# Layer-0 attention of a two-layer graph kernel: scores once, with queries on partitions, instead of twice

## Chip, cores and metric

One core of a Trainium2 chip. The metric is the device time of one execution of the whole kernel, in microseconds (us); lower is better. Engines are named as in the profile: PE (TensorE matmuls; PEld its weight loads), DVE (VectorE), ACT (ScalarE), POOL (GpSimd), SP (the queue that issues the DMAs).

## The reference, cut to what matters

Sixteen samples of 512 nodes and 256 features go through two layers. Layer 0 is masked attention with 8 heads of 32, a residual and a layer norm; layer 1 is attention with one head whose logits are a sum of a query part and a key part.

```python
q, k, v = proj(Wq, bq), proj(Wk, bk), proj(Wv, bv)           # x @ W.T + b, 8 heads of 32
scores = einsum('bhqd,bhkd->bhqk', q, k) / sqrt(32)
scores = where(adj + eye > 0, scores, -inf)
out = einsum('bhqk,bhkd->bhqd', softmax(scores), v)          # -> (b, n, 256)
h = layernorm(x + out @ Wo.T + bo) * gamma + beta
f = h @ fc_w.T + fc_b                                        # layer 1
logits = (f @ q_w.T + q_b) + (f @ k_w.T + k_b).T
masked = logits + (1 - adj) * -1e9
masked = where(masked >= 0, masked, 0.01 * masked)
y = softmax(masked) @ f + h
```

## The kernel before, in words

Every matrix that must be exact to float32 is split in a high and a low part of type float32r; a product of two such is three matmuls (`three_terms`, L387). The 32 columns of a head's q and k are stacked three times on partitions by SBUF-to-SBUF DMAs (`stack`, L272, into `q_stack` and `k_stack`: high, low and high against high, high and low), so that one matmul of 96 rows gives the exact scores of a head.

Layer 0 computes the scores twice. A first pass (L534, `sm_bank`) has queries on partitions, in one float32r term, from a copy of q with the other heads' rows at zero (`q_pad`, filled by DMAs); DVE adds the mask and takes the maximum of each query's row (L928, one instruction and the read of its accumulator). The maxima are turned on PE (`turn_max`), negated and sent by DMA to a 97th row of `q_stack`. The second pass (L524 or L521, `st_bank`) has keys on partitions and the maximum already subtracted by that row; the mask is added by a bfloat16 matmul with a turned mask (L526) or, in 5 of 32 tiles, by DVE (L921); ACT takes the exponential (L708) into `e`, where it is already the moving operand for the product with v (`times_v`, L462, float32, four heads side by side, 32 columns of the array each). The sums of the exponentials run over partitions: POOL adds the four key tiles (`add_e`, L1009), PE multiplies the sum by ones (`total`, L472), DVE takes reciprocals of 128x512 (L856) and POOL multiplies the head outputs by them (L1014) and forms their low part (L1018).

Both passes have 32 tiles of 128x512 a sample (8 heads by 4 blocks of 128), two PSUM banks each; the product with v has one, and three banks are shared in turn by all else. The order of everything is written out by hand: each engine runs a loop over t (one step for each sample, with one step before and two after), in it a loop over 32 positions s. A position has one tile of either pass and the pieces placed there; a piece has an offset, as (15, "op0", -1) for the output projection of the sample before. The maxima of a sample run 21 tiles ahead of its exponentials (`LEAD`), the attention of layer 1 runs two samples behind. Engines take their instructions strictly in order and wait for each other by semaphores whose counts follow from these lists (`Signal`).

In one position PE runs:

```python
nc.tensor.matmul(bank, k_stack[g][:, i, kt*P:(kt+1)*P], q_stack[g][:, i, :], start=True, stop=False)  # L524
nc.tensor.matmul(bank, ident_b, mask_t[par][:, kt, :], start=False, stop=True)                         # L526
nc.tensor.matmul(sm_bank[s % 2], q_pad[j//GH][:, j%GH, qt*P:(qt+1)*P], kt_hi[j//GH], ...)              # L534
```

L526 and L534 are followed by the pieces of that position: transposes of x, of the normalised h and of layer 1's exponentials (L399, L481, L495), the projections q, k, v, op (output) and fc, the key logits kb (all L387), the product with v, the sums, the turned mask (L439) and layer 1's product (`attend`, L505). Other lines in the rows: ACT's copies out of PSUM (L651), its copies with a bias (L674), layer 1's exponential with the sum of its row (L646); POOL's layer-1 mask (L1047); DVE's small reciprocal (L941).

Of the kernel before, what the change touches and what calls it, by code (L numbers as in the profile page):

```python
# [29 lines left out]
P = 128  # L30
# [6 lines left out]
POS = NG * NT * GH  # L37
# [7 lines left out]
DVE_MASKED = (12, 14, 15, 26, 29)  # L45
LEAD = 21

FIRST, LAST = -1, NB + 1


def on(t, off):

    return 0 <= t + off < NB


class Signal:
# [9 lines left out]
    def after(self, step, t):  # L66
        last = self.place[step]
        return self.by * sum(min(max(t + off + (n <= last), 0), NB) for n, off in enumerate(self.offs))

PE_STEPS = [
# [6 lines left out]


OFF = {name: off for _, name, off in PE_STEPS}
FILLS = [name for _, name, _ in PE_STEPS if not name.startswith("pv")]
# [6 lines left out]
    "at1": ("dve", "fin1"), **{f"et{c}": ("act", f"et{c}") for c in range(NT)},  # L90
    **{f"m{j}": ("dve", f"m{j}") for j in range(NG)}}
ACT_STEPS = [
# [5 lines left out]
DVE_STEPS = [  # L98
# [5 lines left out]
POOL_STEPS = [  # L104
    ("sum1_3a", -1), ("sum1_3b", -1), ("x_bo", -1), ("o_norm0", -1), ("diag", 1), ("sum0_1a", 0), ("o_lo0", -1),
    ("sum0_1b", 0), ("sum0_2a", 0), ("sum0_2b", 0), ("o_norm1", -1), ("l_mask", -1), ("o_lo1", -1), ("sum0_3a", 0),
    ("sum0_3b", 0), ("neg_mean", -1), ("var_eps", -1), ("rstd", -1), ("shift", -1), ("sum1_1a", 0), ("sum1_1b", 0),
    ("h_gamma", -1), ("h_rest", -1), ("sum1_2a", 0), ("sum1_2b", 0)]


def maxima_tile(s):

    n = s - (POS - LEAD) if s >= POS - LEAD else s + LEAD
    return (1 if s >= POS - LEAD else 0), n // NT, n % NT


def build(nc, x, adj, wq, bq, wk, bk, wv, bv, wo, bo, gamma, beta, fc_w, fc_b, q_w, q_b, k_w, k_b, out):
    with ExitStack() as ctx:  # L118
# [24 lines left out]
        ident_b = sb("ident_b", [P, P], BF16)  # L143
        ones = sb("ones", [P, DH])
# [9 lines left out]
        mask_t = [sb(f"mask_t{i}", [P, NT, N], BF16) for i in range(2)]  # L154
# [7 lines left out]
        q_stack = [sb(f"q_stack{g}", [STACK + 1, GH, N], F32R) for g in range(NG)]  # L162
        k_stack = [sb(f"k_stack{g}", [STACK + 1, GH, N], F32R) for g in range(NG)]
        v = sb("v", [P, NT, D])
        row_max = sb("row_max", [P, NH, NT])
        neg_max = sb("neg_max", [GH * NT, NG, P], F32R)
        e = sb("e", [P, NT, GH, N])
        e_sum = sb("e_sum", [P, GH, N])
        q_pad = [sb(f"q_pad{g}", [P, GH, N], F32R) for g in range(NG)]
# [3 lines left out]


        o_raw = [sb("o_raw0", [P, N]), x_in[:, 2:4, :].rearrange("p c d -> p (c d)")]
        recip = [sb("recip0", [P, N]), x_in[:, 0:2, :].rearrange("p c d -> p (c d)")]
# [7 lines left out]
        rstd = sb("rstd", [P, NT])  # L184
        feat = sb("feat", [P, NT, D])
        z = sb("z", [P, NT, N + 2])
        scratch = e[:, :, :, :].rearrange("p c g n -> p (c g) n")
# [52 lines left out]
        def program(iteration):  # L240

            for t in range(FIRST, LAST + 1):
                iteration(t, t % 2)
# [855 lines left out]
```

## Time and profile before

| | |
|---|---|
| median of 3 runs (lowest, highest) | 1097.93 us (1094.98, 1108.29) |
| the profiled execution, its own time | 1106.9 us |
| its span, first to last instruction | 1104.8 us |
| mean granted TensorE clock | 0.971 of 2.4 GHz |
| instructions | 16668 |
| DMA, mean of the 16 engines | 109 GB/s |

The busy time of PE is a union of modelled durations: a matmul's duration has its way through the array in it, and the next one starts before it ends. What a stretch of matmuls costs is therefore read as the difference of two start times. The same holds in part for ACT and DVE, where an instruction starts some 0.1 us before the one ahead of it has ended.

### The profile page before, as it was taken

To read this page: it belongs to the slowest core of one execution; us is meant where nothing else is said; L and a number is where in the kernel's file an instruction comes from. 1 tells how busy PE (TensorE), PEld (TensorE's weight loads), DVE (VectorE), ACT (ScalarE), POOL (GpSimd) and SP (SyncE) were. 2 spreads that over 40 slices of the span, in tenths; PEclk is the share of its full clock that TensorE was granted. 3 is DMA by queue.
4 is the path that set the end of the run, shared out by engine and by line. 5 is a ranking of instruction groups with operands and counts; after the bars stand their busy time and mean duration, and the time that the engine had idled before them with its cause. 6 is when DMAs were issued, how large, how long until landed. Compare 5 with 4: busy or idle time off the path is not lost. (4 is left out here: it accounts for less than half of the span.)

```text
span 1104.8 us, 16668 instructions
## 1 busy us (share of the span) xinstructions
PE 1021.8 (92%) x5720; PEld 649.2 (59%) x5720; DVE 782.6 (71%) x1945; ACT 622.8 (56%) x1180; POOL 722.8 (65%) x415
## 2 busy tenths in 40 slices
PE   5789899999999999999999998999999999999866
PEld 4445565656656565665666564666656566665454
DVE  4667777877767787777778777777767767775432
ACT  2145466565646557575655657564555746566633
POOL 3056787675667667666777766576766657778740
PEclk9899999999999999999999999999989999999978
DMA  5677827576564667667374767646366663745010
GB/s 133 106 123 145 133 73 143 102 144 96 113 116 89 135 113 144 96 121 127 102 134 83 153 115 137 103 103 119 79 141 105 136 108 99 135 76 90 29 48 28
DMA packets 81571, 120.89 MB, mean 109 GB/s; under 512 B 9296, under 2 KB 36432, under 8 KB 81488
## 3 DMA queue, kind: packets, MB, share of 16 engines
q1 hardware_dynamic: 81488, 119.84, 56.8%
q8 instruction: 46, 0.75, 0.3%
q14 instruction: 37, 0.30, 0.1%
HBM read 52.44 MB, written 8.39 MB: 55 GB/s over the span
## 5 line engine op out<-in xcount | busy, mean ns | idle before, releaser
L708 ACT ACTIVATE e<-st_bank 128x512 f32<-128x512 f32 x512 | 307.4, 602 | 404.1 <-PE st_bank L526 223.5
L928 DVE CUSTOM_DVE_ANT_0 sm_bank<-sm_bank,masks 128x512 f32<-128x512 f32 x512 | 354.1, 693 | 155.3 <-PE sm_bank L534 152.2
L1009 POOL TENSOR_TENSOR e_sum<-e_sum,e 128x1024 f32<-128x1024 f32 x128 | 303.7, 2385 | 49.8 <-ACT e L708 49.8
L534 PE MATMUL sm_bank<-kt_hi,q_pad 128*128 128x512 f32 x512 | 281.9, 552 | 32.9 <-issue 28.0
L524 PE MATMUL st_bank<-q_stack,k_stack 97*128 97x512 f32 x432 | 197.7, 458 | 3.8 <-ACT e L708 3.0
L1009 POOL TENSOR_TENSOR e_sum<-e 128x1024 f32<-128x1024 f32 x64 | 152.2, 2378 | 67.9 <-ACT e L708 61.1
L526 PE MATMUL st_bank<-mask_t,ident_b 128*128 128x512 bf16 x432 | 169.2, 392 | 0.0
L524 PEld LDWEIGHTS st_bank<-q_stack,k_stack 97*128 97x128 f32 x432 | 81.5, 189 | 111.5 <-ACT e L708 103.3
L462 PE MATMUL o_bank<-e,v 128*32 128x512 f32 x1024 | 136.4, 605 | 0.7 <-ACT e L708 0.7
L505 PE MATMUL shared<-feat,z 128*128 128x256 f32 x512 | 134.5, 412 | 1.4 <-ACT z L651 1.4
L534 PEld LDWEIGHTS sm_bank<-kt_hi,q_pad 128*128 128x128 f32 x512 | 103.2, 202 | 44.5 <-issue 31.8
L505 PEld LDWEIGHTS shared<-feat,z 128*128 128x128 f32 x512 | 105.7, 209 | 18.7 <-ACT z L651 2.2
L526 PEld LDWEIGHTS st_bank<-mask_t,ident_b 128*128 128x128 bf16 x432 | 42.0, 97 | 81.7 <-issue 73.4
L1034 POOL TENSOR_SCALAR_AFFINE_SELECT masks<-masks 128x512 bf16<-128x512 bf16 x16 | 10.2, 639 | 119.8 <-DVE masks L911 119.8
L921 DVE TENSOR_TENSOR st_bank<-st_bank,mask_t 128x512 f32<-128x512 f32 x80 | 56.0, 701 | 34.8 <-PE st_bank L521 33.7
L387 PE MATMUL shared<-weight_hi,split_hi 128*128 128x256 f32 x256 | 73.7, 288 | 6.0 <-POOL split_lo L1018 6.0
L387 PE MATMUL shared<-weight_hi,split_lo 128*128 128x256 f32 x256 | 72.7, 284 | 0.0
L928 DVE DVE_READ_ACCUMULATOR2_ANT row_max<- 128x1 f32 x512 | 72.6, 142 | 0.0
L387 PE MATMUL shared<-weight_lo,split_hi 128*128 128x256 f32 x256 | 72.6, 283 | 0.0
L856 DVE RECIPROCAL recip<-recip 128x128 f32<-128x128 f32 x64 | 60.5, 946 | 12.8 <-ACT recip L651 12.7
L856 DVE RECIPROCAL x_in<-x_in 128x128 f32<-128x128 f32 x64 | 60.2, 945 | 4.5 <-ACT x_in L651 4.5
L387 PE MATMUL shared<-xt_hi,weight_hi 128*128 128x512 f32 x128 | 53.2, 416 | 2.5 <-DVE xt_lo L838 1.8
(131 smaller groups left out, 1836.7 us busy)
## 6 DMA issues: line engine op xcount, KB each, us to landing
adj_in<-in_adj SPq DMA_DIRECT2D x32, 1024.0 KB, 7.8
q_stack<-qt_hi SPq DMA_DIRECT2D x64, 256.0 KB, 9.7
k_stack<-kt_hi SPq DMA_DIRECT2D x64, 256.0 KB, 8.8
x_in<-in_x SPq DMA_DIRECT2D x16, 512.0 KB, 10.4
q_pad<-qt_hi SPq DMA_DIRECT2D x128, 64.0 KB, 7.7
q_stack<-qt_lo SPq DMA_DIRECT2D x32, 256.0 KB, 8.6
k_stack<-kt_lo SPq DMA_DIRECT2D x32, 256.0 KB, 11.9
h<-in_x SPq DMA_DIRECT2D x16, 512.0 KB, 3.8
```

The lines of the kernel that those rows point to most:

```text
L387: last = nc.tensor.matmul(bank, a, b, start=(kt == 0 and n == 0), stop=(kt == kts - 1 and n == 2))
L462: last = nc.tensor.matmul(o_bank[i * DH:(i + 1) * DH, :], v[:, kt, o:o + DH], e[:, kt, i, :], start=(kt == 0), stop=(kt == NT - 1))
L505: last = nc.tensor.matmul(bank[:, k * D:(k + 1) * D], z[:, c, kt * P:(kt + 1) * P], feat[:, kt, :], start=(kt == 0), stop=(kt == NT - 1))
L524: nc.tensor.matmul(bank[:, :], k_stack[g][:, i, kt * P:(kt + 1) * P], q_stack[g][:, i, :], start=True, stop=False)
L526: nc.tensor.matmul(bank[:, :], ident_b[:, :], mask_t[par][:, kt, :], start=False, stop=True).then_inc(st_done.sem, 1)
L534: nc.tensor.matmul(sm_bank[s % 2][:, :], q_pad[j // GH][:, j % GH, qt * P:(qt + 1) * P], kt_hi[j // GH][:, :], start=True, stop=True).then ...
L708: nc.scalar.activation(e[:, kt, i, :], st_bank[s % 2][:, :], ACT.Exp, scale=SCALE)\
L856: last = nc.vector.reciprocal(recip[g][:, n], recip[g][:, n])
L921: nc.vector.tensor_tensor(st_bank[s % 2][:, :], st_bank[s % 2][:, :], mask_t[par][:, kt, :], ALU.add)\
L928: nc.vector.tensor_tensor_reduce(sm_bank[s % 2][:, :], sm_bank[s % 2][:, :], mask[nxt if off else par][:, qt * N:(qt + 1) * N], 1.0, LOWES ...
L1009: nc.gpsimd.tensor_tensor(e_sum[:, pair, :], a, b, ALU.add).then_inc(pool_done.sem, 1)
L1034: nc.gpsimd.affine_select(out=mask_diag[nxt], in_=mask_diag[nxt], compare_op=ALU.not_equal, fill=0.0, base=0, pattern=[[0, NT], [-1, P]], ...
```

## The change

- The scores are computed once, as tiles of 128 queries by 512 keys, exact, from the stacks of 96 rows (the 97th row, `q_pad`, the first pass, the mask matmul, the turned mask and the turned maxima go). The weights and the bias of q carry -1/sqrt(32), so the masked minimum is taken.
- DVE adds the mask and takes the minimum of each row in place; ACT computes exp(min - x) with a bias from a column and sums each row as it goes (`accum_out`); DVE takes the reciprocal of 128 sums; POOL multiplies the tile by them; PE turns the tile, four float32 transposes of 128x128; ACT (22 of 32) or DVE (10 of 32) copies it to `e_t`. The distances: reciprocal one position behind, transposes and copy three behind; `e` holds four tiles, the scores have two banks, the turned tiles two, the shared ones stay three.
- The product with v runs four times a sample, each over 4 key tiles and 4 heads with 256 queries, where it ran eight times over 4 heads with 512. Its result is already normalised: ACT makes the high part from its bank, DVE the low part. `add_e`, `total`, the 128x512 reciprocals and POOL's two steps go.
- Steps of POOL on h (residual bias, gamma, rest) and its layer-1 mask are cut in four.
- All pieces are placed anew, by position and offset in one number (position = number mod 32, samples behind = number div 32).

```diff
+TURN = 3
+ROOM = 4
+RECIP = 1
+SCORED = 2
+TURNED = 2
+SHARED = 3
+DVE_COPIED = (0, 1, 2, 4, 12, 13, 22, 25, 29, 31)
+PE_AT = {
+    "v1": 0, "v0": 2, "et0": 67, "pv3": 37, "et3": 71, "xt0": -25, "at2": 71, "at3": 73, "xt1": -23, "op0": 42,
+    "op1": 43, "et1": 76, "q0": -20, "at0": 77, "at1": 79, "k0": -16, "ht1": 50, "ht0": 50, "pv0": 18, "fc0": 51,
+    "fc1": 53, "kb": 54, "pv1": 23, "k1": -7, "q1": -3, "pv2": 30, "et2": 63}
+SP_AT = {
+    "x": -32, "stack1": 1, "store1": 66, "store0": 73, "x_again": 15, "stack0": -13, "adj": -12, "adj_again": 24}
...
+            def scores(s, b):
+                g, i, qt = tile(s)
+                if s % (TILES // NG) == 0:
+                    pe.wait_ge(stacked[g].sem, stacked[g].of(f"stack{g}", b))
+                u, earlier = ago(s, SCORED)
+                pe.wait_ge(exp_done.sem, exp_done.of(u, b + earlier))
+                nc.tensor.matmul(sm_bank[(TILES * b + s) % SCORED][:, :], q_stack[g][:, i, qt * P:(qt + 1) * P], k_stack[g][:, i, :],
+                                 start=True, stop=True).then_inc(sm_done.sem, 1)
+            def turn(u, b):
+                pe.wait_ge(scaled.sem, scaled.of(u, b))
+                w, earlier = ago(u, TURNED)
+                copied = dve_copied if w in DVE_COPIED else act_copied
+                pe.wait_ge(copied.sem, copied.of(w, b + earlier))
+                n = TILES * b + u
+                for c in range(NT):
+                    last = nc.tensor.transpose(et_bank[n % TURNED][:, c * P:(c + 1) * P], e[:, n % ROOM, c * P:(c + 1) * P], ident[:, :])
+                last.then_inc(turned.sem, 1)
...
+            def exponential(s, b):
+                u, earlier = ago(s, ROOM)
+                act.wait_ge(min_done.sem, min_done.of(s, b))
+                act.wait_ge(turned.sem, turned.of(u, b + earlier))
+                n = TILES * b + s
+                k = n % ROOM
+                nc.scalar.activation(e[:, k, :], sm_bank[n % SCORED][:, :], ACT.Exp, scale=-1.0, bias=row_min[:, k:k + 1],
+                                     accum_out=row_sum[:, k:k + 1]).then_inc(exp_done.sem, 1)
...
+            def masked_minima(s, b):
+                qt = tile(s)[2]
+                if s == 0:
+                    dve.wait_ge(pool_done.sem, pool_done.of("diag", b))
+                dve.wait_ge(sm_done.sem, sm_done.of(s, b))
+                n = TILES * b + s
+                bank, k = sm_bank[n % SCORED], n % ROOM
+                nc.vector.tensor_tensor_reduce(bank[:, :], bank[:, :], mask[b % 2][:, qt * N:(qt + 1) * N], 1.0, -LOWEST,
+                                               ALU.add, ALU.min, row_min[:, k:k + 1])\
+                    .then_inc(min_done.sem, 1)
+            def reciprocal(u, b):
+                dve.wait_ge(exp_done.sem, exp_done.of(u, b))
+                k = (TILES * b + u) % ROOM
+                nc.vector.reciprocal(row_recip[:, k:k + 1], row_sum[:, k:k + 1]).then_inc(recip_done.sem, 1)
...
+            def normalise(s, b):
+                pool.wait_ge(recip_done.sem, recip_done.of(s, b))
+                k = (TILES * b + s) % ROOM
+                nc.gpsimd.tensor_scalar(e[:, k, :], e[:, k, :], row_recip[:, k:k + 1], None, ALU.mult).then_inc(scaled.sem, 1)
```

In a position PE runs the scores, then the transposes of three tiles before, ACT the copy of three before, then the exponential, DVE the minimum, then the reciprocal of one before and the copy of three before, with the pieces of the position between or after them.

## Rows read from the trace of the kernel before

**Rows 1.** The page, part 1: busy us and share of each engine.

```profile
PE 1021.8 (92%) x5720; PEld 649.2 (59%) x5720; DVE 782.6 (71%) x1945; ACT 622.8 (56%) x1180; POOL 722.8 (65%) x415
```

**Rows 2.** Windows: busy us of each engine, granted clock, DMA share, GB/s.

```profile
182.00:243.00 61.00, 59.79 (x350) 37.55 (x348) 47.63 (x119) 38.44 (x73) 42.70 (x25) 1.00 0.61 110
...
792.00:853.00 61.00, 58.17 (x313) 35.51 (x312) 43.82 (x109) 35.68 (x68) 38.74 (x23) 0.94 0.62 116
...
1036.00:1105.00 69.00, 43.45 (x218) 33.24 (x216) 21.51 (x60) 26.62 (x54) 26.30 (x17) 0.85 0.13 42
```

**Rows 3.** Timeline of PE, one tile: start us, duration us, instruction.

```profile
511.71 0.39 PE L524 MATMUL st_bank<-q_stack,k_stack 97*128 97x512 f32 x1
511.94 0.39 PE L526 MATMUL st_bank<-mask_t,ident_b 128*128 128x512 bf16 x1
511.98 0.59 PE L534 MATMUL sm_bank<-kt_hi,q_pad 128*128 128x512 f32 x1
512.41 0.28 PE L387 MATMUL shared<-weight_hi,split_hi 128*128 128x256 f32 x1
```

**Rows 4.** Timeline of PE, four float32 transposes and a layer-1 product.

```profile
525.38 0.60 PE L481 MATMUL shared<-ident,h 128*128 128x128 f32 x4
525.82 1.89 PE L505 MATMUL shared<-feat,z 128*128 128x256 f32 x8
527.36 0.59 PE L524 MATMUL st_bank<-q_stack,k_stack 97*128 97x512 f32 x1
```

**Rows 5.** Timeline of PE, the product of four heads with v.

```profile
516.71 1.07 PE L462 MATMUL o_bank<-e,v 128*32 128x512 f32 x8
517.71 0.50 PE L524 MATMUL st_bank<-q_stack,k_stack 97*128 97x512 f32 x1
```

**Rows 6.** Lines by form: busy us, mean ns of one, idle us.

```profile
L472 PE MATMUL shared<-e_sum,ones 128*32 128x512 f32 x256 | 34.1, 605 | 1.4 <-POOL e_sum L1009 1.4
L1047 POOL TENSOR_SCALAR adj_in<-adj_in 128x2048 f32<-128x2048 f32 x16 | 30.4, 1900 | 3.2 <-DMA adj_in<-in_adj 1.9
L1014 POOL TENSOR_TENSOR x_in<-x_in 128x512 f32<-128x512 f32 x16 | 20.4, 1272 | 5.2 <-DVE x_in L856 5.2
```

**Rows 7.** Timeline of ACT: copy, copy with bias, exponential with a sum.

```profile
511.57 0.58 ACT L651 COPY z<-shared 128x512 f32<-128x512 f32 x1
512.04 0.71 ACT L674 ACTIVATE qt_hi<-shared,bias_col 128x512 fp32r<-128x512 f32 x1
512.62 0.61 ACT L708 ACTIVATE e<-st_bank 128x512 f32<-128x512 f32 x1
...
551.33 0.76 ACT L646 ACTIVATE z<-z,l_negmax 128x512 f32<-128x512 f32 x1
...
552.04 0.64 ACT L708 ACTIVATE e<-st_bank 128x512 f32<-128x512 f32 x1
```

**Rows 8.** Timeline of DVE: masked maximum and a small reciprocal.

```profile
503.80 0.69 DVE L928 CUSTOM_DVE_ANT_0 sm_bank<-sm_bank,masks 128x512 f32<-128x512 f32 x1
...
504.41 0.17 DVE L941 RECIPROCAL l_recip<-l_sum 128x4 f32<-128x4 f32 x1
```

**Rows 9.** Timeline: first, third, sixteenth sample, last tile, last output projection.

```profile
53.52 0.47 PE L524 MATMUL st_bank<-q_stack,k_stack 97*128 97x512 f32 x1 [0.16 <-issue]
...
161.73 0.60 ACT L708 ACTIVATE e<-st_bank 128x512 f32<-128x512 f32 x1 [0.29 <-PE st_bank L526]
...
992.72 0.60 ACT L708 ACTIVATE e<-st_bank 128x512 f32<-128x512 f32 x1 [0.29 <-PE st_bank L526]
...
1044.51 0.50 PE L524 MATMUL st_bank<-q_stack,k_stack 97*128 97x512 f32 x1
...
1062.02 0.39 PE L387 MATMUL shared<-weight_hi,split_hi 128*128 128x256 f32 x1 [1.23 <-POOL split_lo L1018]
```

**Rows 10.** Timeline of SP, then its DMA to landing, first 60 us.

```profile
32.60 0.60 SPq L278 DMA_DIRECT2D k_stack<-kt_lo  x1
...
k_stack<-kt_lo SPq DMA_DIRECT2D x2, 256.0 KB, 12.8
```

More of the change, by code:

```diff
@@ L64, in __init__, with of, all @@
         assert len(self.place) == len(steps)
-    def after(self, step, t):
+    def of(self, step, b):
         last = self.place[step]
+        t = b - self.offs[last]
         return self.by * sum(min(max(t + off + (n <= last), 0), NB) for n, off in enumerate(self.offs))
-PE_STEPS = [
[6 rows of a table removed]
-OFF = {name: off for _, name, off in PE_STEPS}
-FILLS = [name for _, name, _ in PE_STEPS if not name.startswith("pv")]
+    def all(self, name, b):
+        return max(self.of(step, b) for step in self.place if step[:-1] == name and step[-1].isdigit())
+FILLS = [name for name, _ in steps(PE_AT) if not name.startswith("pv") and name not in ("at1", "at3")]
+BANK = {name: n % SHARED for n, name in enumerate(FILLS)}
+BANK["at1"], BANK["at3"] = BANK["at0"], BANK["at2"]
 READ_BY = {
@@ L223, in build @@
[L223 to L224 removed]
+        shared = [pb(f"shared{i}") for i in range(SHARED)]
+        bank_of = {name: shared[n] for name, n in BANK.items()}
+        tiles = [(s, 0) for s in range(TILES)]
+        sm_done = Signal(sem("sm_done"), tiles)
+        min_done = Signal(sem("min_done"), tiles)
+        exp_done = Signal(sem("exp_done"), tiles)
@@ new lines, in build @@
+        recip_done = Signal(sem("recip_done"), [ago(s, RECIP) for s in range(TILES)])
+        scaled = Signal(sem("scaled"), tiles)
+        turned_tiles = [ago(s, TURN) for s in range(TILES)]
+        turned = Signal(sem("turned"), turned_tiles)
+        act_copied = Signal(sem("act_copied"), [u for u in turned_tiles if u[0] not in DVE_COPIED])
+        dve_copied = Signal(sem("dve_copied"), [u for u in turned_tiles if u[0] in DVE_COPIED])
+        pe_done = Signal(sem("pe_done"), steps(PE_AT))
@@ new lines, in times_v, with turn_h @@
+                        last = nc.tensor.matmul(o_bank[i * DH:(i + 1) * DH, 2 * half * P:2 * (half + 1) * P], v[:, kt, o:o + DH],
+                                                e_t[:, k % 2, kt, i, :], start=(kt == 0), stop=(kt == NT - 1))
+                last.then_inc(pe_done.sem, 1)
+            def turn_h(kt, b):
+                pe.wait_ge(act_done.sem, act_done.all("hn", b))
+                pe.wait_ge(*bank_read(f"ht{kt}", b))
+                bank = bank_of[f"ht{kt}"]
+                for c in range(NT):
+                    last = nc.tensor.transpose(bank[:, c * P:(c + 1) * P], h[b % 2][:, c, kt * P:(kt + 1) * P], ident[:, :])
+                last.then_inc(pe_done.sem, 1)
@@ new lines, in attend @@
+            def attend(c, b):
+                k = c % 2
+                pe.wait_ge(act_done.sem, max(act_done.of(f"et{c}", b), act_done.all("feat", b)))
+                if k == 0:
+                    pe.wait_ge(*bank_read(f"at{c}", b))
+                bank = bank_of[f"at{c}"]
+                for kt in range(NT):
+                    last = nc.tensor.matmul(bank[:, k * D:(k + 1) * D], z[:, c, kt * P:(kt + 1) * P], feat[:, kt, :],
+                                            start=(kt == 0), stop=(kt == NT - 1))
+                last.then_inc(pe_done.sem, 1)
@@ new lines, in o_high, with normal_rows @@
+            def o_high(g, b):
+                act.wait_ge(pe_done.sem, max(pe_done.of("kb", b - 1), pe_done.all("fc", b - 1)))
+                copy(o_hi[:, g, :], f"pv{2 * g + 1}", o_bank[:, :], b)
+            def normal_rows(half, b):
+                act.wait_ge(pool_done.sem, pool_done.of("shift", b))
+                for c in range(2 * half, 2 * half + 2):
+                    last = nc.scalar.activation(h[b % 2][:, c, :], h[b % 2][:, c, :], ACT.Identity, bias=shift[:, c:c + 1],
+                                                scale=rstd[:, c:c + 1])
+                last.then_inc(act_done.sem, 1)
@@ new lines, in query_logits @@
+            def query_logits(half, b):
+                dve.wait_ge(act_done.sem, act_done.of(f"feat{half}", b))
+                dve.wait_ge(pe_done.sem, pe_done.all("at", b - 1))
+                for k in range(2):
+                    c = 2 * half + k
+                    last = nc.vector.tensor_tensor_reduce(z[:, c, 0:D], bank_of[f"fc{half}"][:, k * D:(k + 1) * D], qw_row[:, :],
+                                                          1.0, logit_bias[:, 3:4], ALU.mult, ALU.add, q_dot[:, c:c + 1])
+                last.then_inc(done, 1)
```

1162 lines of the change are left out of this document (516 added, 646 removed), and 29 rows, old and new, of tables (ACT_AT, ACT_STEPS, DVE_AT, DVE_STEPS).

## Prediction

> **What bounds the kernel now.** I read the page first: PE is busy 1021.8 of 1104.8 us, 92%, DVE 71%, POOL 65%, ACT 56% [rows 1]. Then the windows: in a full stretch of 61 us at clock 1.00 PE is busy 59.8, DVE 47.6, POOL 42.7, ACT 38.4 [rows 2]. PE sets the pace. Its durations overlap, so I worked from start times. Tile starts: L524 at 511.71, the piece behind its three matmuls at 512.41, so a tile with the mask matmul costs 0.70 us back to back, about 0.235 a matmul of 512 columns [rows 3]. A layer-1 product of eight instructions costs 1.54, four transposes 0.44 [rows 4], four heads' product with v 1.00 [rows 5], and the sums over partitions are of the same form (605 ns, 8 instructions) [rows 6]. For a sample: 27 tiles at 0.75 (0.70, and some have an entry from a float32 group) and 5 at 0.50 make 22.8; q and k 24 matmuls at 0.235, 5.6; v, op and fc 72 half-width ones at 0.118, 8.5; kb 6 at 0.235, 1.4; layer 1's product 4 x 1.54, 6.2; its, x's and h's 32 transposes at 0.11, 3.5; v-product 8 x 1.05 with its entries, 8.4; sums 2.1; turned mask and maxima about 1.1. Together 59.6. The samples are 63.9 us apart: the third sample's first exponential is at 161.73, the sixteenth's at 992.72, 830.99/13 [rows 9]. So 4.3 us a sample are waits and lower clock. The rest of the span: the first tile starts at 53.52, from the last tile (1044.51) to the end it is 60.3 us [rows 9].
>
> **The change on PE, where it counts.** Per sample it removes 32 score matmuls at 0.235 (7.5), 27 mask matmuls (6.3), the sums (2.1), the turned mask and maxima (1.1). It adds 128 float32 transposes. Four of them cost 0.44 from start to start [rows 4], so 32 x 0.44 = 14.1. The new position is then 0.235 + 0.44 = 0.68, 21.6 a sample against 22.8 for the old tiles. A switch from float32r scores to float32 transposes may cost more: at worst a score matmul has left the array before the next group starts, 0.39 instead of 0.235 [rows 3], which is 0.16 x 32 = 5.0 more. At best nothing. I take nothing, because groups of float32 and float32r follow each other in rows 4 with no such gap, and keep 5.0 for the range. The v-product has the same columns in 64 half-width steps: 4 heads, 512 columns, cost 1.00, so 256 cost 0.50 at least, 16 x 0.50 = 8.0 less shared entries, against 8.4; if weight loads of 32 columns don't hide under half the columns, each step costs up to 0.65, 2.4 more, the other end. I take 7.6. New sum: 21.6 + 5.6 + 8.5 + 1.4 + 6.2 + 3.5 + 7.6 = 54.4, 5.2 under the old.
>
> **ACT.** Removed: the copies of the sums, of the turned mask and of the head output. Added: the exponential gets a bias column and a sum. A plain copy holds ACT 0.47, one with a bias column 0.58, an exponential with bias and sum 0.71 (551.33 to 552.04, read from SBUF) [rows 7]; the plain exponential is of the first kind. So 0.60 to 0.71, I take 0.68: 32 x 0.68 = 21.8. 22 copies at 0.47, 10.3. The rest of its pieces (4 logits 2.6, 4 exponentials 2.8, 4 turned tiles 1.9, norm 2.0, ten copies 4.8, q and k 2.3) 16.4. Sum 48.5, from 36 to 38 of busy time before [rows 2].
>
> **DVE.** Minimum 0.61 from start to next start, its accumulator read beside it [rows 8]: 19.5. Ten copies at 0.61, 6.1; 32 reciprocals of one column, up to 0.17 each [rows 8], 4.5. Its other pieces add to 17: 47, as before (the large reciprocals and masked tiles go).
>
> **POOL.** 32 multiplications of 128x512 by a column. A tensor_scalar of four times the width takes 1.90, a tensor_tensor of this width 1.27 [rows 6], so 0.48 to 1.27; I take 0.6, the nearer kind, with a start cost. 19.2, with 13.5 for h, the mask and the norm 33, in place of 42. At 1.27 it would be 54, and nearly the bound.
>
> **What now waits.** The two score banks are the loop: scores(s) waits for exp(s-2). A round is matmul 0.5, minimum 0.61 + 0.14, exponential about 0.9 with its sum, four hand-overs at about 0.1: 2.5 to 2.6 us for two tiles. Behind that wait on PE stand the transposes and all pieces of the position. Where both positions are full PE needs 2.8 or more for two and the wait is over before; where neighbours are empty it needs 1.36. By the placement positions 26 to 28 are empty on PE and 3 and 4 nearly so: there PE waits about 1.3 and 1.0 us a sample. Single empty ones leave 0.2 to 0.3 for what ACT has ahead of the exponential (a copy, 0.47), another 1.2. Transposes come three positions behind (5.6 us), the chain to them takes about 4, so no wait as long as POOL takes 0.6. The clock and small waits I leave at 2. So 54.4 + 1.3 + 1.0 + 1.2 + 2 = 59.9, 60 us a sample.
>
> **SP.** Every DMA of `q_pad` (8 a sample) and of the maxima goes; the stacks, x, adj and stores stay. stack0 is issued at position 19 for the next sample, 13 positions or 24 us ahead; its six DMAs take 3.9 us to issue and up to 12.8 to land [rows 10]. stack1 has 15 positions. adj_again stands in SP from position 24 until the next masks are made at 31; behind it are only x and stack1 of the next turn. I cost this at nothing; if that cover went, the first scores of a head group would be late by what is missing of 17 us.
>
> **Ends.** The first tile no longer waits for maxima. It waits for stack0, whose last DMA is issued at 32.60 and lands in 12.8, at 45 [rows 10], against 53.52. The first two samples took 108.2 to 161.73 [rows 9]; without layer 1's and then the output's pieces the new loop gives 43 and 51, 94. The last sample, with nothing to prepare, 53 (before 51.8). The end: before, the last output projection starts at 1062.02 [rows 9], 17.5 after the last tile, with sum, reciprocals and POOL's two steps in it; now about 9.5 (transpose, copy, product, two halves). The 42.8 behind it stay. 52.3.
>
> Sum: 45 + 94 + 13 x 60 + 53 + 52 = 1024 against 1104.8; with the 2.1 us around the span 1026 against 1106.9. That execution lies 0.8% above the median, so for a median 1026 x 1097.9/1106.9 = 1018 us, 7.3% faster.
>
> **Rivals.** Time = (244 + 13 P + 2) x 0.992 with P the us between samples.
> (1) PE closes up: few waits, P = 57: 979 to 980 less 4 for lighter ends, about 975. For it: the other engines need under 49. Against: two banks and strict order.
> (2) The gain goes into the switch between scores and transposes: 5.0 a sample on PE, P = 65: 1082. For it: no row shows float32r scores straight before transposes of data that had long been there.
> (3) Slower, by the score loop: the exponential stands on ACT behind all that is placed there. The bare loop is 16 x 2.6 = 42 a sample; if ACT's 16.4 of pieces and half of DVE's 17 and half the ACT copies lie in it and not beside it, P = 42 + 16 + 8.5 + 5 = 71.5, 1166. It decides from a round of 3.75 us (2 x 60/32); equal to the kernel before at 4.0. Against: heavy PE positions give the others time.
> (4) Slower, by the clock. Transposes take 17.6 of 60 us, so the other matmuls only 37 to 38, 62%; in the window from 1036, where PE was busy 63% of the time, the clock was 0.85 [rows 2]. There 30% of the time is at 1.2 GHz, where half-width matmuls start 0.21 apart instead of 0.118. P = 54.4/(1 - 0.3 x 0.45) + 5 = 68: 1121. Against: the transposes here keep PE busy in time, and in rows 4 they run at full speed in their places. The Trainium skill ("TensorE: Matmul & The Clock Gate", Part 4: PE-mode transpose) says that transposes don't count as PE-busy in the way that brings the full clock, which is this rival; the trace has too few transposes to bear it out.
> (5) POOL's multiplication costs 1.27: P about 63: 1057.
> (6) The change doesn't do what it says, that is, the deleted matmuls weren't on the path. Rows 1 speak against it.
>
> **Chances.** Forecast (P 58.5 to 63, with rival 5 in it) 0.54; (1) 0.18; (2) 0.10; (3) 0.10; (4) 0.06; (6) 0.02. Likeliest 1018. The range from 965 (rival 1 with P = 56) to 1085 (rival 2) leaves (3) and (4) out, 0.16. This kernel can be told from no change at about 2%, 1076 us. Faster: 0.54 + 0.18 and part of (2) and (3), 0.77; same 0.11; slower 0.12.
>
> **What would show it.** Right: L534's successor and one matmul a tile on PE, starts of scores and transposes 0.68 apart when nothing waits; four transposes 0.44; exponentials 0.68 apart back to back; POOL at 0.6; first tile near 45; 60 between samples; PE busy near 90%, and its waits for exponentials at positions 26 to 28 and 4. Wrong: a clock under 0.95; transposes at 0.6 or more for four; PE waiting for exponentials at most positions; POOL above 1.0 and PE waiting for it; waits of PE for the stacks at positions 0 or 16.

## The result, and the profile after

The changed kernel takes 1145.7 us (four runs, 1144.6 to 1147.6), 1.040 times the time before, 95% interval 1.035 to 1.046: slower, where 1018 us was forecast in a range of 965 to 1085. The page of after, parts 1 and 4 (busy us and share of each engine; the chain of work that ended last, by engine), beside [rows 1]:

```profile
PE 979.0 (86%) x7304; PEld 770.4 (67%) x7304; DVE 763.9 (67%) x2412; ACT 824.6 (72%) x1948; POOL 1013.0 (88%) x856
...
POOL 61%; PE 24%; DVE 6%; issue 3%; ACT 2%; DMA 1%; SPq 1%; DVEq 0%; ACTq 0%
```

PE did get its work cut. But POOL, at 65% before, is now the busiest engine, and the last chain runs through it. The windows of after (columns as in [rows 2]):

```profile
182.00:243.00 61.00, 54.51 (x435) 43.07 (x434) 43.82 (x140) 47.69 (x115) 58.27 (x51) 1.00 0.54 110
...
792.00:853.00 61.00, 53.85 (x422) 42.53 (x420) 43.32 (x136) 46.69 (x112) 58.29 (x50) 0.97 0.55 113
```

In the first of these windows PE is busy 54.5 of 61 us, where it had 59.8, and POOL 58.3, where it had 42.7. What POOL does, in the lines by form of after:

```profile
L1013 POOL TENSOR_SCALAR e<-e,row_recip 128x512 f32<-128x512 f32 x512 | 805.0, 1581 | 52.7 <-DVE row_recip L888 45.9
L998 POOL TENSOR_TENSOR h<-h,gamma_row 128x256 f32<-128x256 f32 x64 | 46.7, 730 | 5.9 <-PE shared L449 4.1
...
L993 POOL TENSOR_SCALAR adj_in<-adj_in 128x512 f32<-128x512 f32 x64 | 39.6, 619 | 5.3
```

The multiplication of one tile takes 1581 ns; the layer-1 mask, also a tensor_scalar and of the same shape, takes 619. The waits (engine, line, releaser: us in total, times, longest) show who waits behind it:

```profile
DVE sm_bank L881 <- PE sm_bank L483: 204.3, 179, 11.0
PEld et_bank L493 <- POOL e L1013: 191.6, 218, 1.8
ACT e_t L652 <- PE et_bank L493: 123.6, 159, 3.7
PE et_bank L493 <- POOL e L1013: 120.8, 172, 1.6
```

PE's transposes wait for POOL, ACT's copies for PE, DVE's minima for the scores that stand behind those transposes on PE: one releaser, passed on. The timeline at the points of [rows 9]: the first sample's first scores, first exponential of the third and of the sixteenth sample, last scores, and last output projection:

```profile
44.58 0.79 PE L483 MATMUL sm_bank<-k_stack,q_stack 96*128 96x512 f32 x1 [11.34 <-DMA k_stack<-kt_lo]
...
165.65 0.69 ACT L660 ACTIVATE e<-sm_bank,row_min 128x512 f32<-128x512 f32 x1 [1.91 <-DVE row_min L881]
...
1029.20 0.69 ACT L660 ACTIVATE e<-sm_bank,row_min 128x512 f32<-128x512 f32 x1 [1.65 <-DVE row_min L881]
...
1091.44 0.50 PE L483 MATMUL sm_bank<-k_stack,q_stack 96*128 96x512 f32 x1
...
1106.48 0.47 PE L385 MATMUL shared<-weight_hi,split_hi 128*128 128x256 f32 x1
```

The samples are (1029.20 - 165.65)/13 = 66.4 us apart, where 60 was forecast and 63.9 measured before. Put together by the forecast's own terms: start 44.6, first two samples 121.1, thirteen at 66.4, last 62.2, end 53.3, together the span of 1144.7.

### The profile page after: what moved, and what is told of

Read it like the earlier page. It is cut to its first block, busy times and chain, and to the rows that moved or that the text cites. A ratio compares the mean times of both kernels' runs of the same rounds, so it can differ in the third digit from the quotient of the medians.

```text
span 1144.7 us, 22568 instructions
## 1 busy us (share of the span) xinstructions
PE 979.0 (86%) x7304; PEld 770.4 (67%) x7304; DVE 763.9 (67%) x2412; ACT 824.6 (72%) x1948; POOL 1013.0 (88%) x856
## 4 chain that ended last, share of the span: by engine, by line
POOL 61%; PE 24%; DVE 6%; issue 3%; ACT 2%; DMA 1%; SPq 1%; DVEq 0%; ACTq 0%
POOL e L1013 48%; PE shared L385 10%; PE et_bank L493 6%; POOL h L998 3%; PE shared L473 3%; POOL h L1003 3%; POOL adj_in L993 2%; DVE sm_bank L881 2%; POOL h L973 2%; PE sm_bank L483 2%; DVE z L864 2%; POOL rstd L985 1%; PE shared L449 1%; DMA k_stack<-kt_lo 1%; PE shared L463 1%
## 5 line engine op out<-in xcount | busy, mean ns | idle before, releaser
L1013 POOL TENSOR_SCALAR e<-e,row_recip 128x512 f32<-128x512 f32 x512 | 805.0, 1581 | 52.7 <-DVE row_recip L888 45.9
L493 PE MATMUL et_bank<-ident,e 128*128 128x128 f32 x2048 | 326.1, 282 | 123.2 <-POOL e L1013 120.8
L660 ACT ACTIVATE e<-sm_bank,row_min 128x512 f32<-128x512 f32 x512 | 357.8, 702 | 64.4 <-DVE row_min L881 61.5
L493 PEld LDWEIGHTS et_bank<-ident,e 128*128 128x128 f32 x2048 | 239.5, 143 | 214.8 <-POOL e L1013 191.6
L652 ACT COPY e_t<-et_bank 128x512 f32<-128x512 f32 x352 | 208.3, 592 | 123.7 <-PE et_bank L493 123.6
L483 PE MATMUL sm_bank<-k_stack,q_stack 96*128 96x512 f32 x512 | 249.7, 488 | 13.8 <-DMA k_stack<-kt_lo 11.3
L483 PEld LDWEIGHTS sm_bank<-k_stack,q_stack 96*128 96x128 f32 x512 | 98.8, 193 | 48.9 <-issue 25.1
L894 DVE COPY e_t<-et_bank 128x512 f32<-128x512 f32 x160 | 109.4, 684 | 26.4 <-PE et_bank L493 24.2
L440 PE MATMUL o_bank<-e_t,v 128*32 128x256 f32 x2048 | 125.5, 386 | 0.0
L660 ACT ACTIVATION_READ_ACCUMULATOR e<-sm_bank,row_min 128x1 f32 x512 | 108.2, 211 | 0.0
```

The costliest lines, as they stand in the source:

```text
L440: last = nc.tensor.matmul(o_bank[i * DH:(i + 1) * DH, 2 * half * P:2 * (half + 1) * P], v[:, kt, o:o + DH], e_t[:, k % 2, kt, i, :], start ...
L483: nc.tensor.matmul(sm_bank[(TILES * b + s) % SCORED][:, :], q_stack[g][:, i, qt * P:(qt + 1) * P], k_stack[g][:, i, :], start=True, stop=T ...
L493: last = nc.tensor.transpose(et_bank[n % TURNED][:, c * P:(c + 1) * P], e[:, n % ROOM, c * P:(c + 1) * P], ident[:, :])
L652: nc.scalar.copy(turned_to(u), et_bank[(TILES * b + u) % TURNED][:, :].rearrange("p (c n) -> p c n", c=NT)).then_inc(act_copied.sem, 1)
L660: nc.scalar.activation(e[:, k, :], sm_bank[n % SCORED][:, :], ACT.Exp, scale=-1.0, bias=row_min[:, k:k + 1], accum_out=row_sum[:, k:k + 1] ...
L894: nc.vector.tensor_copy(turned_to(u), et_bank[(TILES * b + u) % TURNED][:, :].rearrange("p (c n) -> p c n", c=NT))\
```

## Experiments

Each is an edit of the changed kernel, or of one that is named. "Period" is the time from one sample to the next in the profiled run, from the third sample's first exponential to the sixteenth's, divided by 13; the changed kernel has 66.4 us. "Idle time" is POOL's, in gaps over 0.1 us, for each sample. Times are medians, of four runs in most cases, of ten in e12 and e16 and of one in e5; the kernel before, measured anew beside them, took 1093 to 1101 us.

### What one multiplication costs, and what it decides

**e1: a constant in place of the column.**

```diff
-nc.gpsimd.tensor_scalar(e[:, k, :], e[:, k, :], row_recip[:, k:k + 1], None, ALU.mult)
+nc.gpsimd.tensor_scalar(e[:, k, :], e[:, k, :], 0.03125, None, ALU.mult)
```

> The changed kernel with GpSimd's multiplication of each tile of exponentials by a constant in the place of the column of reciprocals; it leaves out the softmax's division, and keeps every wait, transfer and place. Theory (GpSimd bounds the changed kernel, through 32 multiplications a sample of 1.58 us where the prediction had 0.6): one multiplication falls to about 0.62 us, GpSimd to some 35 us a sample, and the sample from 66.4 us to 57 to 60 us, what TensorE's own 54.4 us and its waits make; the whole execution to 1013 to 1055 us (14 periods shorter than 1144.7). Rival (the score loop over two banks and the new places of the pieces bound it, GpSimd's busy time is only a wait passed on): at most 1.5 us a sample less, 1125 us or more. Rival (GpSimd's column operand is not what is dear, any multiplication of this shape in place is): still 1.58 us each and 1145 us.

1159.0 us, 1.058 times before: that the column is what is dear is refuted, and the last rival holds (any multiplication of this shape in place is dear). The line of the multiplication in e1:

```profile
L1013 POOL TENSOR_SCALAR e<-e 128x512 f32<-128x512 f32 x512 | 769.9, 1504 | 81.7 <-DVE row_recip L888 44.6
```

Its recorded duration is a little shorter, but two in a row start 1.567 us apart (median), against 1.541 with the column. 32 x 0.026 = 0.8 us a sample more; the period went from 66.4 to 67.1. This is a first sign that the period follows POOL.

**e2: a product with the repeated column.**

```diff
+nc.gpsimd.tensor_tensor(e[:, k, :], e[:, k, :], row_recip[:, k:k + 1].to_broadcast([P, N]), ALU.mult)
```

> The changed kernel with the same multiplication written as a product of two tensors, the second one the reciprocal's column repeated along the row; computes the reference. Theory (a scalar operand read from a column is what is dear on GpSimd): the product takes about 1.27 us as GpSimd's other product of this shape did in the kernel before, so GpSimd has 32 x 1.3 + 15 = 57 us a sample, and the sample is 59 to 62 us, 1040 to 1085 us in all. Rival (any operation of GpSimd with a second operand is at the same pace here): 1.5 to 1.6 us each and 1135 to 1150 us. Rival (the bound is the score loop): 1125 us or more whatever it costs.

1007.1 us, 0.920 times before (0.912 to 0.928), below the range expected. It computes the same and takes 12% less than the changed kernel, by one instruction's form. Its line and a window:

```profile
L1013 POOL TENSOR_TENSOR e<-e,row_recip 128x512 f32<-128x512 f32 x512 | 537.1, 1053 | 175.4 <-DVE row_recip L888 170.1
```

```profile
182.00:243.00 61.00, 60.15 (x484) 49.28 (x477) 48.77 (x154) 53.01 (x128) 48.98 (x56) 1.00 0.61 124
```

POOL has fallen to 49.0 of 61 us and PE stands at 60.2: the bound is back at PE, the period is 58.0 us.

**e5: a price list.** Tile s of a sample is multiplied, added to or copied in form s mod 8, each on its own line.

```diff
+if s % 8 == 0:   last = nc.gpsimd.tensor_scalar(ek, ek, col, None, ALU.mult)                 # L1015
+elif s % 8 == 1: last = nc.gpsimd.tensor_scalar(ek, ek, col, 1.0, ALU.mult, ALU.mult)        # L1017
+elif s % 8 == 2: last = nc.gpsimd.tensor_scalar(ek, ek, 0.0, col, ALU.add, ALU.mult)         # L1019
+elif s % 8 == 3: last = nc.gpsimd.tensor_scalar(ek, ek, 0.0, 0.03125, ALU.add, ALU.mult)     # L1021
+elif s % 8 == 4: last = nc.gpsimd.tensor_scalar(ek, ek, 0.0, None, ALU.add)                  # L1023
+elif s % 8 == 5: last = nc.gpsimd.tensor_tensor(ek, ek, ek, ALU.mult)                        # L1025
+elif s % 8 == 6: last = nc.gpsimd.tensor_scalar(ek, ek, 0.5, 0.0625, ALU.mult, ALU.mult)     # L1027
+elif s % 8 == 7: last = nc.gpsimd.tensor_copy(ek, ek)                                        # L1029
```

> A price list: the changed kernel in which GpSimd treats its tiles in eight forms by turns, each on a line of its own, 64 of each: (0) times a column, one operation; (1) times a column, times 1.0; (2) plus 0.0, times a column; (3) plus 0.0, times a constant, the form of the layer-1 mask; (4) plus 0.0 alone; (5) the product of the tile with itself as two tensors; (6) times a constant, times a constant; (7) a copy. Forms 3 to 7 leave out the softmax's division. Known so far for 128x512: form 0 1.58 us, times a constant alone 1.50, tensor product with a repeated column 1.05, plus then times constants (on the adjacency) 0.62. Theory A (an instruction with one operation is slow, with two fast): forms 1, 2, 3, 6 near 0.62, form 4 at 1.5. Theory B (the first operation decides, a multiplication is slow): forms 0, 1, 6 at 1.5, forms 2, 3, 4 near 0.62. Theory C (this tile is slow, by what else reads and writes it, and the mask's tile is not): all forms at 1.0 to 1.6, form 3 too.

The lines by form of e5:

```profile
L1015 POOL TENSOR_SCALAR e<-e,row_recip 128x512 f32<-128x512 f32 x64 | 100.6, 1572 | 43.5 <-DVE row_recip L888 43.5
L1023 POOL TENSOR_SCALAR e<-e 128x512 f32<-128x512 f32 x64 | 98.2, 1534 | 40.1 <-DVE row_recip L888 40.1
L1025 POOL TENSOR_TENSOR e<-e 128x512 f32<-128x512 f32 x64 | 73.0, 1141 | 7.6 <-DVE row_recip L888 7.6
L1017 POOL TENSOR_SCALAR e<-e,row_recip 128x512 f32<-128x512 f32 x64 | 44.5, 695 | 1.9 <-DVE row_recip L888 0.3
L1019 POOL TENSOR_SCALAR e<-e,row_recip 128x512 f32<-128x512 f32 x64 | 44.5, 695 | 12.5 <-DVE row_recip L888 10.8
L1027 POOL TENSOR_SCALAR e<-e 128x512 f32<-128x512 f32 x64 | 39.8, 622 | 10.1 <-DVE row_recip L888 7.3
L1021 POOL TENSOR_SCALAR e<-e 128x512 f32<-128x512 f32 x64 | 39.8, 621 | 62.4 <-DVE row_recip L888 62.4
L1029 POOL COPY e<-e 128x512 f32<-128x512 f32 x64 | 39.2, 612 | 57.2 <-DVE row_recip L888 57.1
```

Theory A (the number of operations decides) holds alone. Both tensor_scalar lines with one operation take over 1.5 us, addition and multiplication alike; all four with two take 0.62 to 0.70. By recorded durations a column in place of a constant costs 0.04 to 0.07 more; with one operation the distance of starts (e1) doesn't bear that out. It is not the tile, since the same tiles are quick in other forms, and not the kind of operation. Why one operation is the slow form no run here shows.

**e7: the same multiplication in two operations.**

```diff
-nc.gpsimd.tensor_scalar(e[:, k, :], e[:, k, :], row_recip[:, k:k + 1], None, ALU.mult)
+nc.gpsimd.tensor_scalar(e[:, k, :], e[:, k, :], row_recip[:, k:k + 1], 1.0, ALU.mult, ALU.mult)
```

> The changed kernel with each multiplication as one instruction of two operations, times the column, times 1.0; computes the reference. Theory A (one operation slow, two fast): about 0.7 us each, GpSimd 37 us a sample; TensorE's 54.4 us and its waits on the scores and on ACT stay, and the period is 56.5 to 58 us, 985 to 1007 us in all. Theory B or C (the operation or the tile decides): 1.5 to 1.6 us each, 1140 to 1160 us.

990.6 us, 0.905 times before (0.899 to 0.910), 13.5% less than the changed kernel: the best of all. Its line, and its window in which PE is busy 60.45 of 61 us:

```profile
L1013 POOL TENSOR_SCALAR e<-e,row_recip 128x512 f32<-128x512 f32 x512 | 370.3, 724 | 323.6 <-DVE row_recip L888 319.4
```

```profile
182.00:243.00 61.00, 60.45 (x482) 50.35 (x482) 49.91 (x165) 53.91 (x129) 38.23 (x56) 1.00 0.63 122
```

The period is 57.0 us. POOL has 38.2 of 61 us and waits for the reciprocals; ACT, the next busiest after PE, has 53.9.

### Does POOL's time count one for one?

**e6: the cheaper form of e2 in 8 of 32 tiles** (`if s % 4 == 1`).

> The changed kernel with 8 of a sample's 32 multiplications (every fourth tile, from tile 1) as a product with the repeated column, the other 24 as they were; computes the reference. The two forms start the next instruction 1.541 and 0.996 us later, so GpSimd has 8 x 0.545 = 4.4 us a sample less. Theory (GpSimd's own time sets the sample's period one for one, until TensorE takes over at 58.0 us): 66.4 - 4.4 = 62.0 us a sample, 1145 - 14 x 4.4 = 1083 us, 1075 to 1092. Rival (as three tiles taken off GpSimd gave a third of their time only, the period follows at a third): 64.9 us, 1124 us.

1083.3 us, period 62.4: 4.0 of 4.4 us counted, as the theory had it.

**e3: three multiplications (tiles 5, 15, 26) on VectorE**, behind the reciprocal; PE's transposes wait for the engine that did the tile.

```diff
+DVE_SCALED = (5, 15, 26)
...
+nc.vector.tensor_scalar(e[:, k, :], e[:, k, :], row_recip[:, k:k + 1], None, ALU.mult).then_inc(dve_scaled.sem, 1)
```

> The changed kernel with 3 of a sample's 32 multiplications (tiles 5, 15 and 26) on VectorE, right behind the reciprocal, and the other 29 on GpSimd as they were; computes the reference. Theory (GpSimd is the bound, so its time comes off one for one): the sample gets 3 x 1.55 = 4.7 us shorter, 61.8 us, and the whole 1075 to 1090 us. Rival (the score loop): less than 1.5 us a sample, 1125 us or more; were VectorE's or ACT's chain the bound, the three operations added to VectorE would make it longer, 1145 us or more.

1125.6 us, period 64.9: 1.5 of 4.7 us. The theory missed; the result lies at the very edge of the rival (1125 or more), though POOL, not the score loop, is what PE still waits for. **e4: the sixteen odd tiles there.**

> The changed kernel with every second multiplication (the odd tiles) on VectorE, right behind the reciprocal; computes the reference. Theory: GpSimd falls to 16 x 1.55 + 15 = 40 us a sample and bounds nothing; VectorE has 43.1 us and 16 operations of 0.3 to 0.6 us more, 48 to 53 us, under TensorE's 54.4 us, so the sample is 57 to 60 us and the whole 1013 to 1055 us. Rival (score loop): 1125 us or more. Rival (VectorE pays as much for a column operand as GpSimd): VectorE has 68 us and the kernel takes 1165 us or more.

1049.6 us, 0.959 times before, in the expected range; the period of 60.5 lies a little above the 57 to 60 expected. VectorE is busy 87% of the span and takes 658 ns for a multiplication, where 300 to 600 was assumed.

**e8: e3 with tiles 6, 18 and 30.** They were chosen by POOL's idle time behind each tile, over eight samples (2.1 us a sample in the changed kernel, 5.1 in e3).

> As the run with three one-operation multiplications on VectorE, but of tiles 6, 18 and 30 in place of 5, 15 and 26; computes the reference. There the trace had GpSimd idle 5.2 us a sample against 2.3 before, 1.7 of it ahead of the product with gamma that stands behind tile 15 and waits for TensorE, 0.9 behind tile 4. Theory (GpSimd's time counts one for one where it has a backlog, and is lost where its next piece waits for another engine): the idle time stays near 2.3 us, the sample gets 4 to 4.6 us shorter, 62 us, and the whole 1080 to 1092 us. Rival (VectorE's added work is what ate two thirds of the gain, wherever the tiles are): 64.9 us and 1125 us again.

1134.5 us, period 65.7: theory and rival both missed, the choice was worse, and the idle time 5.9 us. **e14: the same three multiplied by no engine.**

> The changed kernel in which tiles 6, 18 and 30 are not multiplied by any engine (their softmax's division is left out); the other 29 are multiplied on GpSimd in one operation as before. GpSimd has 4.6 us a sample less, as when VectorE did these three (65.6 us a sample, 1134 us). Theory (the ring over three tiles keeps GpSimd from running ahead, whoever does the three): little better than 1134 us, 1115 to 1135. Rival (VectorE's three operations of 0.66 us, each ahead of a minimum, gave the gain back): 61.8 to 62.5 us a sample, 1080 to 1092 us.

1131.7 us, period 65.6, the same as e8's: VectorE's added work isn't what ate the gain. **e15: the same three on POOL, in two operations.**

> The changed kernel with tiles 6, 18 and 30 multiplied on GpSimd as all others, but in the form of two operations; computes the reference. GpSimd has only 3 x (1.54 - 0.70) = 2.5 us a sample less, not 4.6 as when VectorE did them. Theory (time taken off GpSimd counts one for one while it stays within what the ring lets it run ahead): 63.9 us a sample, 1110 us, 1100 to 1118, better than with the same three on VectorE (1134). Rival (these three places are no good for a gain, or each gain counts at a third): 65.6 us, 1130 us or more.

1133.7 us, period 65.8: only 0.6 of 2.5 us; the theory missed, its rival on the places holds. **e16: e15 with tiles 1, 13 and 25.**

> The changed kernel with the two-operation form in tiles 1, 13 and 25, in place of tiles 6, 18 and 30 (1134 us, 65.7 us a sample, GpSimd's idle time up from 2.3 to 3.9 us); computes the reference. In the run with the cheaper form in every fourth tile from tile 1, GpSimd's idle time did not grow behind tiles 1, 13 and 25. Theory (a cut counts in full at tiles behind which the next reciprocals are long made, and is lost where the ring is tight already): idle time near 2.3 us, 66.4 - 2.5 = 63.9 us a sample, 1105 to 1116 us. Rival (three single cuts are lost in any place, a cut counts only when spread evenly): 65.5 us and 1130 us or more.

1097.7 us, period 63.45: 3.0 us for a cut of 2.5, idle time 1.7. The same cut, in other places, takes four times as much off the whole (48 us against 12). The timeline of e15 at tile 18 shows how a cut is lost (L1014 is the two-operation form):

```profile
596.97 0.28 PE L385 MATMUL shared<-weight_hi,split_lo 128*128 128x256 f32 x1
...
597.80 0.40 PE L483 MATMUL sm_bank<-k_stack,q_stack 96*128 96x512 f32 x1
597.83 0.70 POOL L1014 TENSOR_SCALAR e<-e,row_recip 128x512 f32<-128x512 f32 x1
...
598.23 0.70 DVE L881 CUSTOM_DVE_ANT_0 sm_bank<-sm_bank,masks 128x512 f32<-128x512 f32 x1 [1.31 <-PE sm_bank L483]
...
598.85 0.16 DVE L888 RECIPROCAL row_recip<-row_sum 128x1 f32<-128x1 f32 x1
...
599.11 1.57 POOL L1016 TENSOR_SCALAR e<-e,row_recip 128x512 f32<-128x512 f32 x1 [0.57 <-DVE row_recip L888]
```

POOL is done with tile 18 at 598.5, but the reciprocal of tile 19 is only started at 598.85: on VectorE it stands behind the minimum of tile 20, which waited 1.31 us for scores that stood on PE behind a projection. It is a ring: multiplication of a tile, its transposes, the scores four tiles on, their minimum, the reciprocal of the tile before them, and that tile's multiplication, three tiles after the first. Where PE has a long piece in it, one turn is longer than POOL's own work: here from tile 16 (started at 593.92) to tile 19 it took 5.2 us, of which POOL was busy 4.4. The trace of the changed kernel tells the good places beforehand: there the reciprocal of the tile behind each cut of e16 (tiles 2, 14 and 26) had been ready for 1.75, 2.39 and 1.52 us when POOL came to it, of the tile behind each cut of e15 (7, 19 and 31) for 1.00, 0.39 and 0.09, and of tile 8 for 0.28 (means of eight samples). One cut is 0.84 us. Two sets of three tiles bear this reading out; it wasn't tested on a third. Such a backlog in e16, at tile 1, with tiles 2 and 3 started without idle time:

```profile
543.75 0.69 POOL L1014 TENSOR_SCALAR e<-e,row_recip 128x512 f32<-128x512 f32 x1
544.41 0.73 POOL L998 TENSOR_TENSOR h<-h,gamma_row 128x256 f32<-128x256 f32 x1
545.12 3.10 POOL L1016 TENSOR_SCALAR e<-e,row_recip 128x512 f32<-128x512 f32 x2
```

### The length of the ring, and what is left

**e12: e8 with the transposes and the copy four tiles behind (`TURN = 4`) and five tiles of room in `e` (`ROOM = 5`).**

> The run with the one-operation multiplications of tiles 6, 18 and 30 on VectorE, with the transposes four tiles behind the scores in place of three, and five buffers of exponentials in place of four; computes the reference. There GpSimd stood idle some 1.5 us ahead of the tile behind each of the three: its next reciprocal was not made, since that stands on VectorE behind a minimum, that behind a score, and that on TensorE behind the transposes of the tile three before, which wait for GpSimd's own multiplication. Theory (this ring through all four engines, three tiles long, keeps GpSimd from running ahead, so taking single tiles off it gives little): with a ring of four tiles the idle time of 5.8 us a sample falls to 2 to 3, the sample from 65.6 to 62 us and the whole from 1134 to 1080 to 1095 us. Rival (VectorE's own 0.66 us for each ahead of the next minimum is what holds GpSimd): 1120 us or more.

1100.5 us, 34 us less than e8 where 40 to 54 was expected; idle time 5.9 to 3.9 us, period 64.0. The waits of e8 for POOL and for ACT's exponentials, and under them those of e12:

```profile
PEld et_bank L496 <- POOL e L1023: 168.4, 216, 1.8
PEld sm_bank L485 <- ACT e L663: 23.0, 30, 1.5
```

```profile
PEld et_bank L496 <- POOL e L1023: 29.9, 54, 1.8
PEld sm_bank L485 <- ACT e L663: 91.3, 113, 2.5
```

With a ring of four tiles PE's waits for POOL are down to less than a fifth, as the theory has it. Four times as much wait for ACT came in their place, of the kind that e13 shows. The granted clock stood at 0.94 to 0.95 in its windows, and 1.6 us of POOL's idle time stayed behind tile 29, so the shares of what is missing aren't settled.

**e11: e7 with `TURN = 2`.**

> The kernel with two operations an instruction, with a tile's transposes two tiles behind its scores on TensorE, not three; computes the reference. One tile's way from score to transpose is 0.25 + 0.83 + 0.9 + 0.15 + 0.72 = 2.85 us and the waits between engines, two tiles of TensorE's time are 3.56 us. Theory (with the quick multiplication the way fits in, but any other piece on the way comes through): TensorE waits for GpSimd at perhaps half of the tiles, 60 to 64 us a sample, 1030 to 1090 us in all. Rival (three tiles were more than needed): within 1% of 990 us.

1224.1 us, period 71.7, far above the 60 to 64 expected: two tiles, one turn of the ring, take 2 x 71.7/32 = 4.5 us. PE's weight loads wait 283 us for POOL (2.3 in e7), though POOL is busy only 47% of the span. **e13: e7 with `TURN = 4`, `ROOM = 5`.**

> The kernel with two operations an instruction, with the transposes four tiles behind the scores and five buffers of exponentials; computes the reference. With two tiles the ring cost 14.7 us a sample. Theory (with the quick multiplication a ring of three tiles is slack, what is left of TensorE's waits is for ACT's exponentials ahead of the scores): 57.0 us a sample as now, 985 to 995 us. Rival (some of the waits left still come through the ring): 56.3 us or less, 975 to 982 us.

1025.5 us, period 59.1: slower than e7 by 35 us, theory and rival both wrong. The waits of e13, and under them the same one in e7:

```profile
PEld sm_bank L483 <- ACT e L660: 72.1, 122, 1.5
```

```profile
PEld sm_bank L483 <- ACT e L660: 37.1, 77, 1.5
```

PE's scores wait twice as long for ACT's exponentials. The traces show where: each tile's copy has moved one position on together with its transposes. Over ten samples these waits rose from 1.65 to 3.89 us a sample, and 2.34 us of rise stand at the scores of positions 2, 4, 27 and 30 (the others add up to 0.1 less). They wait for the exponentials of tiles 0, 2, 25 and 28, and those are where ACT has a copy directly ahead in e13 that isn't there in e7. The rise of 2.24 us covers the 2.0 us by which the period grew, so by the traces the loss lies in where the copies stand, not in the longer ring; a kernel with `TURN = 4` and the copies placed anew wasn't run. **e9: e7 with tiles 7, 18, 20 and 27 copied by VectorE too.**

> The kernel with two operations an instruction, and four more of the turned tiles' copies (tiles 7, 18, 20 and 27) on VectorE instead of ACT; computes the reference. In the 57.0 us of a sample TensorE has 54.4 and waits some 3.4 us for ACT's exponentials ahead of its scores. Theory (ACT's queue makes these waits): ACT goes from 47 to 45 us a sample, VectorE from 43 to 45.5, the waits to some 2.5 us, the sample to 56.3 us and the whole to 977 to 985 us. Rival (VectorE's minima come later by as much): 57 to 58 us, 988 to 1005 us.

991.7 us, period 57.1: no gain. The waits for ACT came out at 36.3 us against 37.1. In e7 they stand at the scores of positions 5, 26, 27 and 28 alone, behind exponentials with pieces of layer 1 or a copy ahead of them, and none of the four copies taken off ACT is among those. So e9 shows that ACT's load as such doesn't make the waits, not that its queue doesn't; the rival holds only in that nothing was gained.

## Why the prediction was wrong

The step that failed is the one headed POOL: "POOL's multiplication", taken at 0.6 us and bounded at 1.27. It is 1.58 us, 1.541 from start to start. By the forecast's own sum, 32 x 1.541 = 49.3 and the other pieces' 13.6 (forecast 13.5) are 62.9 us a sample, and with 3.1 us of idle time, small gaps counted, 66.0, where 66.4 was measured. POOL bounds the kernel, not PE, and "no wait as long as POOL takes 0.6" lost its condition. The span is 121 us over the forecast: 6.4 us thirteen times, 27 in the first two samples and 9 in the last make 120 of them. In e7, with the quick form, the first two samples still take 7 us more than forecast, so that much of the 27 isn't POOL's.

How it came about: L1047 of [rows 6] was taken as the price of "a tensor_scalar". Its instruction in the code has two operations (plus a constant, times a constant); the new one has one, and the second argument for it is None. I saw a simpler instruction and took it to be no dearer. The upper end came from another kind of instruction, so nothing in the range was the unknown form's price; no row of before has a tensor_scalar of POOL with one operation on a wide tile. With the form that the row was read from, the kernel takes 990.6 us (e7), inside the range and 2.7% under the forecast: the rest of the sum was sound as a whole, in part because two of its misses went against each other (PE's own demand too low, the waits too high, below).

Point by point:
- PE: four transposes 0.44 forecast, 0.36 to 0.42 measured from start to start in e7; v-product 7.6 a sample, measured 7.46. The switch from scores to transposes, rival 2, is there by half: in e7 the two start 0.235 apart where a projection in float32r is ahead of the scores, 0.32 to 0.34 where float32 transposes or a v-product are, the usual case, and 0.42 behind layer 1's product; rival 2 feared 0.39 throughout. [rows 4], on which the forecast took nothing, have no float32r group ahead of a float32 one. The transposes are cheaper by as much, and the whole position takes 0.68 at the lower quarter and 0.74 in the middle, 0.68 forecast. Of the period of 57.0 in e7, PE's records have 0.6 idle and its weight loads wait 1.7 for exponentials, so the demand of 54.4 was low by 1 to 2.
- The waits for exponentials stood where the forecast had them, at positions 26 to 28 (1.3 us a sample forecast, 1.3 in e7) and near 4 (1.0 forecast, 0.4 at position 5); of the other 3.2 us that it added, for single empty positions, clock and small waits, little is to be seen.
- ACT's exponential 0.68 forecast, 0.68 measured; DVE's minimum 0.61 and 0.61. Start 45 and 44.6, end 52.3 and 53.3. These terms were right.
- The score loop (rival 3) is no bound: of 1144.7 us PE's weight loads waited 5.5 for exponentials ahead of scores, and with POOL quick the same loop runs at 57.0. "No wait as long as POOL takes 0.6" holds: in e7 PE's transposes wait 1.2 us for POOL in the whole run. What the forecast did not have is the ring through the transposes; e11 shows how near its edge is.
- Rival 1 (P = 57, 975 us) is what e7 is: P came out at 57.0, and the time 990.6. The first two samples took 101.2 us and not 94, and the factor 0.992 took off another 8: it was read from one profiled execution of before that lay above the median, and e7's own (989.7) doesn't.
- Rival 4, the clock: the windows of after are at 0.97 to 1.00, of e7 at 1.00, with 128 float32 transposes more a sample. The transposes are part of a full PE here (60.45 of 61 us in e7), so a stretch of transposes alone wasn't tested. The Trainium skill's rule ("TensorE: Matmul & The Clock Gate", Part 4: PE-mode transpose) makes nothing slower here; the trace does not agree with the use I made of it.
- Rival 5 had the right engine with the wrong price. At 1.05 us (e2) the kernel takes 1007. Its 1057 for 1.27 looks too high: 40.6 + 13.6 and 3.1 of idle time are 57.3 us, an estimate, against 58.0 in e2; no run has that price.
- Among the signs of error stood "POOL above 1.0 and PE waiting for it". That is what the lines and waits of after show.

The Trainium skill ("GPSIMD Engine Reference", section 4.1, Engine selection) has operations with one input at about line rate on GpSimd, and two-input ones about twice as slow as VectorE. For 128x512 the trace agrees for the two-operation form (0.62 to 0.70 us, VectorE's 0.66 in e4), and does not for one operation (1.53 to 1.57), which here is slower than the product of two tensors (1.05 to 1.14).

## What to carry to other kernels

A price is that of an instruction's whole form: engine, opcode, shape, and how many operations and operands it has. Where the trace has the opcode but not the form, it isn't a bound, and the test is one kernel with the forms side by side. When an engine is the bound, cut its work where it has a backlog: in a strict order a cut is lost where the next operand isn't ready yet (0.6 us gained for 2.5 at three tiles, 3.0 at three others). How long each operand had been ready can be read from the trace before the cut. A change of the distance between two steps also moves what is tied to them, as the copies in e13: what then stands ahead of what has to be looked at anew.

## What of the hardware was not expected

- GpSimd's tensor_scalar on 128x512 float32 in SBUF: 1534 ns (constant) and 1572 ns (column) with one operation, 621 and 695 ns with two, a copy 612 ns. With a second operation, times 1.0, it is more than twice as fast (1572 and 695 ns with the column).
- A product of two tensors took 1053 ns with a repeated column as second input, 1141 with the tile itself as both, 1272 in [rows 6].
- With sixteen multiplications a sample on VectorE (e4), GpSimd's 128x256 pieces took longer, the first line from e4, the second from the changed kernel:

```profile
L1013 POOL TENSOR_TENSOR h<-h,rest_row 128x256 f32<-128x256 f32 x64 | 57.1, 895 | 0.0
```

```profile
L1003 POOL TENSOR_TENSOR h<-h,rest_row 128x256 f32<-128x256 f32 x64 | 46.6, 730 | 0.0
```
